# Three of four softmax sums are split from SBUF, some units after their last addition, and not from the score bank

## The reference, cut to what matters

```python
q = rms_norm(x @ q_w + q_b, nq_s)                    # 16 sequences of 56 rows, 16 heads of 128
k_img, v_img = rms_norm(img @ ki_w + ki_b), img @ vi_w + vi_b      # 257 rows of context
k_txt, v_txt = rms_norm(txt @ k_w + k_b), txt @ v_w + v_b          # 1243 rows of context
out = softmax(q k_img / sqrt(D)) v_img + softmax(q k_txt / sqrt(D)) v_txt
x   = x + out @ o_w + o_b
```

## Time and profile before

| | |
|---|---|
| median of 3 runs | 1863.59 us (1860.93 to 1867.96) |
| the profiled execution | 1862.32 us, span 1860.5 us |
| PE busy | 1723.5 us, 93% of the span |
| PE weight load busy | 1538.9 us, 83% |
| DVE busy | 1333.3 us, 72% |
| POOL busy | 1182.0 us, 64% |
| ACT busy | 983.2 us, 53% |

### The profile page before, as it was taken

How to read it: one execution, slowest core, us unless ns; L and a number is a source line. 1 busy time by engine, 2 the same in 40 slices (tenths; PEclk the granted TensorE clock), 3 DMA queues, 4 the chain that set the end, 5 groups by cost and what they waited for, 6 DMA issues and landing times. The chain is left out here.

```text
span 1860.5 us, 31204 instructions
## 1 busy us (share of the span) xinstructions
PE 1723.5 (93%) x8731; PEld 1538.9 (83%) x8731; DVE 1333.3 (72%) x2561; ACT 983.2 (53%) x1657; POOL 1182.0 (64%) x1053
## 2 busy tenths in 40 slices
PE   7899899999999999999999999999983997799998
PEld 6677688989889889889889889898883886688887
DVE  4454577887887877877878878878763664677777
ACT  3455455565565655655656655665643562344343
POOL 1233578888888888888888888888752331233332
PEclk8999989999999999999999999999996998799999
DMA  3367564566466466555565665664437881233332
GB/s 113 105 236 249 182 182 105 122 126 135 116 123 133 116 120 128 132 116 123 133 124 116 127 139 121 126 134 113 86 86 242 274 266 44 76 116 115 110 117 76
DMA packets 419413, 251.25 MB, mean 135 GB/s; under 512 B 352320, under 2 KB 370880, under 8 KB 417568
## 3 DMA queue, kind: packets, MB, share of 16 engines
q1 hardware_dynamic: 419360, 250.61, 52.8%
HBM read 187.71 MB, written 60.10 MB: 133 GB/s over the span
## 5 line engine op out<-in xcount | busy, mean ns | idle before, releaser
L1362 ACT ACTIVATE p_high<-psum,key_rms 128x448 fp32r<-128x448 f32 x384 | 244.9, 638 | 373.2 <-PE psum L1183 373.1
L1181 PE MATMUL psum<-u_high,c_high 128*128 128x448 f32 x768 | 288.2, 375 | 37.3 <-DVE psum L1456 31.2
L1445 DVE TENSOR_TENSOR p_low<-psum,p_high 128x448 fp32r<-128x448 f32 x384 | 237.1, 617 | 90.8 <-ACT psum L1364 88.8
L1181 PE MATMUL psum<-p_high,c_high 128*128 128x448 f32 (+1 forms) x768 | 283.4, 369 | 2.9 <-DVE p_low L1445 2.9
L1182 PE MATMUL psum<-u_low,c_high 128*128 128x448 f32 x768 | 282.0, 367 | 0.0
L1183 PE MATMUL psum<-u_high,c_low 128*128 128x448 f32 x768 | 281.8, 367 | 0.0
L1183 PE MATMUL psum<-p_high,c_low 128*128 128x448 f32 (+1 forms) x768 | 280.9, 366 | 0.0
L1182 PE MATMUL psum<-p_low,c_high 128*128 128x448 f32 (+1 forms) x768 | 280.9, 366 | 0.0
L1456 DVE COPY psum<-beta_wide 128x448 f32<-128x448 f32 x416 | 259.3, 627 | 20.3 <-DMA beta_wide<-absorbed_biases 4.5
L1661 POOL TENSOR_TENSOR c_low<-stage,c_high 128x512 fp32r<-128x512 f32 x208 | 269.3, 1295 | 0.0
L1364 ACT ACTIVATE psum<-psum,key_rms 128x448 f32<-128x448 f32 x384 | 232.9, 607 | 0.0
(11 more groups left out here) (246 smaller groups left out, 4030.2 us busy)
## 6 DMA issues: line engine op xcount, KB each, us to landing
stage<-in_ctx SPq DMA_DIRECT2D x210, 256.0 KB, 2.8
averages<-o_raw SPq DMA_DIRECT2D x64, 448.0 KB, 5.2
o_stage<-averages SPq DMA_DIRECT2D x32, 896.0 KB, 5.5
u_raw<-absorbed_queries SPq DMA_DIRECT2D x60, 448.0 KB, 5.6
absorbed_queries<-u_stage SPq DMA_DIRECT2D x14, 1792.0 KB, 6.8
beta_wide<-absorbed_biases SPq DMA_DIRECT2D x32, 448.0 KB, 5.2
recip_wide<-reciprocals SPq DMA_DIRECT2D x32, 448.0 KB, 4.0
p_wide<-probs_by_expert SPq DMA_DIRECT2D x32, 448.0 KB, 3.5
```

The costliest lines, as they stand in the source:

```text
L1181: nc.tensor.matmul(out, high, rhigh, start=start, stop=False, **kw)
L1362: nc.scalar.activation(p_high[:, probs_slot(u), :], src, ACT.Exp, scale=key_rms[:, t:t + 1])
L1445: return nc.vector.tensor_tensor(out, a, b, ALU.subtract)
```

## The change

The rows of the sums after units 3, 24 and 25 no longer go through the score bank. At these units the last addition is like any other: it writes `p_sum` in SBUF, and the bank is seeded at once. The rounding and the subtraction are done later by `split_late`, from `p_sum` in SBUF: for unit 24 at step 1 of the next batch ahead of `take(0)`, for unit 25 in the same step behind `take(0)`, and for unit 3 at step 9 behind `take(8)`. Unit 2 stays as it was. In the last batch both text sums are split in the tail, after the last take. Nothing changes on PE, ACT, POOL and SP, and no instruction is added or removed: DVE still does two instructions for each of the four sums.

```diff
+        IN_BANK = [2 * LONE - 2]
+        LATE_IMAGE = 9
...
+            def split_sum(it, u, total):
+                s, half = LAST_ADDS[u]
+                n, at = 4 * it + 2 * s + half, 2 * s + half
+                dve.wait_ge(sum_added, ADDS * it + added(u) + CREDIT["sum_added"])
+                dve.wait_ge(sum_wide, n - 3 + CREDIT["sum_wide"])
+                nc.vector.tensor_copy(p_sum_high[:, at, :], total).then_inc(sum_high_ready, 1)
+                dve.wait_ge(sum_high_ready, n + 1)
+                sub(p_sum_low[:, at, :], total, p_sum_high[:, at, :].bitcast(F32)).then_inc(sum_split, 1)
+
+            def split_late(it, u):
+                s, half = LAST_ADDS[u]
+                split_sum(it, u, p_sum[:, 2 * s + half, :])
...
-                    done = nc.vector.tensor_tensor(part if u in LAST_ADDS else total, part, total, ALU.add)
+                    done = nc.vector.tensor_tensor(part if u in IN_BANK else total, part, total, ALU.add)
                 done.then_inc(sum_added, 1)
-                if u in LAST_ADDS:
-                    n, at = 4 * it + 2 * s + half, 2 * s + half
-                    dve.wait_ge(sum_added, ADDS * it + added(u) + CREDIT["sum_added"])
-                    dve.wait_ge(sum_wide, n - 3 + CREDIT["sum_wide"])
-                    nc.vector.tensor_copy(p_sum_high[:, at, :], part).then_inc(sum_high_ready, 1)
-                    dve.wait_ge(sum_high_ready, n + 1)
-                    sub(p_sum_low[:, at, :], part, p_sum_high[:, at, :].bitcast(F32)).then_inc(sum_split, 1)
+                if u in IN_BANK:
+                    split_sum(it, u, part)
...
-                    if u in LAST_ADDS:
+                    if u in IN_BANK:
                         s, half = LAST_ADDS[u]
                         dve.wait_ge(sum_split, 4 * it + 2 * s + half + 1 + CREDIT["sum_split"])
                     else:
                         dve.wait_ge(sum_added, ADDS * it + added(u) + CREDIT["sum_added"])
                     seed_after(it, u, has_next)
...
+                    if has_prev and step == 1:
+                        split_late(it - 1, UNITS - 2)
                     if step >= 1:
                         take(it, step - 1, has_next)
+                    if has_prev and step == 1:
+                        split_late(it - 1, UNITS - 1)
+                    if step == LATE_IMAGE:
+                        split_late(it, 2 * LONE - 1)
...
             def tail(it):
                 take(it - 1, UNITS - 1, False)
+                for u in (UNITS - 2, UNITS - 1):
+                    split_late(it - 1, u)
```

## The result

| | median | range | runs |
|---|---|---|---|
| before | 1864.76 us | 1860.93 to 1867.96 | 4 |
| changed | 1842.97 us | 1842.46 to 1845.04 | 4 |

The ratio is 0.9886 (95% interval 0.9865 to 0.9907): 21.8 us less by the medians, where 21.6 were forecast. The kernel before has a fourth run here, which moves its median from 1863.59 to 1864.76. The profiled execution of the changed kernel took 1845.04 us, with a span of 1843.3.

A forecast was written before the change was run, and what follows sets the result against it. PE was taken to bound the kernel, busy 901.64 of 928 us. 15 x 1.38 = 20.7 us plus 0.9 for the first batch made 21.6 off 1862.32: 1840.7, or 1842 as median; range 1831 to 1853.

The forecast's parts named there:

- The bank of unit 24: Batch boundary: unit 24's bank is seeded earlier, so PE's stall before unit 0's scores goes whole, 1.16 us.
- norm(0) behind c_twice: Batch boundary on DVE: norm(0) no longer waits for two in-bank splits, follows POOL's c_twice and comes 1.41 us earlier.
- The collision of the moved splits: Between norm(0) and norm(2): SBUF splits and POOL's operations delay each other, so norm(2) gains 0.62 us, not 1.2.
- The bank of unit 3, and unit 5: Unit 6's stall goes and its scores start 1.99 us earlier; PE stands still a little at unit 5.
- What is late next: Unit 8: norm(6) waits for c_twice and comes 1.38 us earlier; PE waits anew, about 0.6 us.
- The pair at step 9 costs nothing: Unit 3's late split before norm(10) ends up to 0.4 us after that norm's time, but PE loses nothing.
- The sum: Whole kernel: 20.7 us from 15 boundaries, 0.9 from the first batch, 0 from the tail; 21.6 us together.
- What stands outside the loop: Time ahead of and behind the loop: the prediction's sum has no term for it.
- collisions cost nothing: Rival: splits slip between POOL's operations, norm(2) 1.22 and norm(6) 1.98 us earlier; 30.7 us gained, 1833; chance 0.17.
- Collisions eat the chain: Rival: norm(2) comes no earlier, only c_twice's slack of 0.76 us before norm(6) is won; 12.4 us, 1851; chance 0.16.
- Nothing moves: Rival: POOL's chain is the period, or unit 0's stall returns in full at unit 1 or 6; 1863; chance 0.07.
- the slower rival: Unit 24's rounding lands behind POOL's long operation, making take(0) and norm(2) late; 10 us slower, 1874; chance 0.05.

The follow-up runs named there:

- both_first: Changed kernel with unit 25's split placed directly behind unit 24's, both ahead of take(0); 1855.56 us, period 71.32 us.
- small25: Changed kernel with unit 25's late split cut to 8 of 448 columns, the rest left out; 1836.71 us, period 70.13 us.
- seed8_first: Changed kernel with unit 8's bank seeded ahead of norm(6) at step 6, the rest of take(5) behind it; 1832.86 us, period 69.95 us.
- small3: Changed kernel with unit 3's late split at step 9 cut to 8 of 448 columns, the rest left out; 1845.25 us, period 70.58 us.
- after_again: The changed kernel run once more, unaltered, in another group of runs; 1843.16 us, period 70.58 us.
- seed8_before: Kernel before, all four sums split in the bank, with unit 8's seed moved ahead of norm(6); 1859.78 us, period 71.71 us.
- image_only: Kernel before with only unit 3's sum split late, at step 9; units 24 and 25 stay in the bank; 1851.77 us, period 71.26 us.

## Why the prediction was right

By its own steps:

- **The bank of unit 24.** Right. The stall of 0.89 is gone.
- **norm(0) behind c_twice.** Right. It waits 0.62 us for c_twice of POOL, where it had waited for nothing but DVE's own backlog.
- **The collision of the moved splits.** Right in kind, and close in sum. The chain from norm(0) to norm(2) was to take 747.45 - 741.18 = 6.27 us and took 6.19. The parts differ: the pair of unit 24 cost POOL 0.24 and not 0.34; with unit 25's pair the subtraction, which started 0.02 us earlier, won, and c_twice took 0.46 more. The hardest reading, POOL held for the whole of a pair, did not come true: key_root ran and ended (732.78) while unit 24's subtraction was still running (732.41 to 733.03). The rounding from SBUF is 0.39 us when it is alone, below the 0.45 of the nearest row; I had put 0.65 into the pair. both_first shows the lock, and small25 what the collision costs: 0.47 us a batch.
- **The bank of unit 3, and unit 5.** Right. Unit 6 starts with no wait, and PE stands 0.27 before unit 5, which the text had named without a size.
- **What is late next.** Right: a new stall at unit 8, 0.68 where "about 0.6" was said, from norm(6) behind c_twice. seed8_first shows that the queueing of the seed behind that norm is the cause: with the seed ahead of it the wait is gone.
- **The pair at step 9 costs nothing.** Right, by small3.
- **The sum.** 15 x 1.37 = 20.6 us for the full batches, as forecast (20.7). From PE's first scores of the loop to its last rounded product with ones it was 1390.24 - 231.63 = 1158.61 us before and 1368.60 - 232.81 = 1135.79 after: 22.8 less. So the first batch and the tail gave 2.2 us, not 0.9. The tail gave nothing, as assumed: the second product of the sums starts 1.63 us behind the first in both kernels. The rest lies at the start: from the first scores to the second issue of the lone tile's transfer it was 91.31 us before and 88.15 after, 3.16 less, where one period gives 1.37. This stretch is not steady, though: after_again has 88.86 and small3 89.93, so much of the excess can be what executions of one kernel differ by.
- **What stands outside the loop.** Taken at nothing, and it was not: in the two profiled executions it took 5.6 us more after the change, 1.2 ahead of the loop and 4.4 behind it. So the profiled execution gained 17.3 us and not 21.6.

The rows behind the loop show where most of the 4.4 us went. First the kernel before, then the changed one:

```profile
1431.07 0.72 POOL L1953 TENSOR_TENSOR ow_low<-v_stage,ow_high 128x256 fp32r<-128x256 f32 x1 [6.20 <-DVE ow_high L1913]
1431.24 2.43 DVE L1917 TENSOR_TENSOR o_low<-o_stage,o_high 128x1792 fp32r<-128x1792 f32 x1 [0.25 <-ACT o_high L1883]
1431.84 0.47 PE L1837 MATMUL psum<-o_high,vw_high 128*128 128x448 f32 x1 [2.43 <-POOL ow_low L1953]
```

```profile
1409.70 2.02 DVE L1936 TENSOR_TENSOR o_low<-o_stage,o_high 128x1792 fp32r<-128x1792 f32 x1
1409.72 2.60 POOL L1972 TENSOR_TENSOR ow_low<-v_stage,ow_high 128x256 fp32r<-128x256 f32 x1 [5.93 <-DVE ow_high L1932]
1412.37 0.53 PE L1856 MATMUL psum<-o_high,vw_high 128*128 128x448 f32 x1 [4.49 <-POOL ow_low L1972]
```

It is the same collision once more, between a subtraction of DVE and one of POOL. Before, POOL came first and PE stood still for 2.43 us. After, DVE came first by 0.02 us, POOL's short operation took 2.60 instead of 0.72, and PE stood still for 4.49. In the 4 us behind that idle PE's granted clock was 0.57, near the lower of its two levels (1.2 and 2.4 GHz), and 12 matmuls started; in the kernel before, in the 4 us from 1431.84, it was 1.00, and 20 started. POOL comes first in the profiles of both kernels that have no late split (before and seed8_before, where the stretch from the loop's last product with ones to the end takes 470.0 us), and DVE in those of all ten that have one (472.5 to 474.6 us). That the change turns the order round is thus likely, but by which path was not followed, and each kernel has one profile only.

**What was luck.** The 1.37 us a batch was forecast by its steps and came by them. That the medians differ by 21.8 where 21.6 were forecast is in part luck: the sum left out the loss behind the loop, and had too little for the first batch; the profiled execution it was worked out for would have been 1840.7 and was 1845.04; the same two kernels in another group of runs differ by 18.6.

Of the rivals, "collisions cost nothing" would have had norm(2) 1.22 and norm(6) 1.98 us earlier, a period of 70.0; it was 70.60, and small25, which removes one of three collisions, has 70.13. "Collisions eat the chain" would have left norm(2) where it was and given 71.2, which is what image_only shows without the moved text sums (71.26). "Nothing moves" did not happen. What kept the slower rival off was the place of unit 24's rounding, 0.36 us behind norm(0), where scale_u comes 1.12 us behind it; both_first shows what a later rounding meets there.

The tail of the changed kernel: the end of DVE's late instructions, ACT's copy of the first sum, and PE's product for the second:

```profile
1367.14 0.62 DVE L1447 TENSOR_TENSOR x_low<-p_sum,p_sum_high 128x448 fp32r<-128x448 f32 x1
...
1367.99 0.52 ACT L1335 ACTIVATE sum_row<-psum 1x448 f32<-1x448 f32 x1
1368.60 0.44 PE L1254 MATMUL psum<-p_sum_high,ones_r 128*128 128x448 f32 x1 [1.05 <-DVE x_low L1447]
```

The bracket names DVE, but its split had ended at 1367.76, 0.84 us before. What ends just ahead of the product is ACT's copy of the first sum out of the one bank (1368.51), so the tail had room for the moved work.

## What to carry to other kernels

A stall of the busiest engine is worth only what the slowest loop through the other engines gives up. Follow that loop (here norm, key_root, the long operation, c_low, c_twice, norm) past the stall before you count its length as a gain: here 2.63 us of stalls gave 1.37. Work moved from PSUM to SBUF on DVE can be shorter alone and still cost more, where POOL is busy: look up what POOL runs at that moment, and place the work behind an event for which POOL itself waits. And once a wait has moved, look at the order of the queue in front of it: a seed queued behind a norm cost 0.63 us a batch and took one exchange of places to mend. Last, compare the stretches that the change does not touch as well: here one behind the loop took 4.4 us more, and the total alone would not have shown it.

## What the runs showed of the hardware

The exclusive access was expected from the earlier trace rows; the runs add how regular it is. In the changed kernel and in both_first, from 300 to 1300 us, every rounding of one SBUF tile to another that was issued while a c_low or scale_u of POOL ran ended 0.24 to 0.27 us after that operation, whether it took 0.52 us or 2.33 (0.39 alone). Every subtraction with two SBUF inputs that was issued during a c_low or c_twice ended 0.48 or 0.49 us after it (0.62 or 0.63 alone). The Trainium skill (page "SBUF — State Buffer", section "Who interferes with whom") says that the later one "fully blocks" for the whole instruction of the other; the trace agrees (2.33 us behind scale_u's 2.28).

The other way round, POOL's operation ends as if it had started about 0.15 us before DVE's recorded end. c_twice of 0.74 us behind the subtraction that ends at 737.20 ends at 737.79, and scale_u of 2.12 us behind the one that ends at 733.03 ends at 735.03. The small key_root (128 x 1, 0.55 us alone, 0.63 behind a rounding) did not hold the subtraction that was issued while it ran: that took 0.62 or 0.63 us in each of the 15 batches.
